# Third stage: the normalisation's DVE steps one tile later, the residual's product on DVE instead of POOL, and POOL's scatters split around the root

## The chip, the cores and the metric

One core of a Trainium2 chip (trn2) runs the whole program. The metric is the device time of one execution in microseconds (us), the median of three runs: 1230.01 us before the change (1229.64 to 1231.98). Engines: PE multiplies matrices, DVE is the vector engine, ACT the activation engine, POOL (GpSimd) also issues the indirect DMAs, SP issues the plain ones.

## The reference, cut to what matters

The layer has an attention block on 16 x 512 tokens of 128 channels, then an encoder layer with a mixture of experts. The part that matters here is the last expression:

```python
# y: [tokens, 128], after the encoder's own attention and first layer norm
idx = argmax(y @ Wg.T)                      # one of 8 experts per token
moe = relu(y @ W1[e] + b1[e]) @ W2[e] + b2[e]      # for each token its own e
z   = layer_norm(y + moe, g2, be2)
x   = x + gb * z                            # gb is kept away from zero: |gb| >= 0.25
```

## The kernel before, in words

The program has three stages: windowed attention, then the encoder's attention with routing, then the experts. The second stage scatters each token's row of 385 floats (y without the layer norm's scale, an index, x plus shift, and the gate `GC`) into a buffer in DRAM sorted by expert (L983). The third stage, from about 1048.7 us of the profiled span, is the one that the change touches.

It walks over 72 tiles (`NS`) of 128 sorted tokens, each of one expert, in 18 quads (`NQX`) of four tiles. The order is written out by hand on each engine:

- SP loads the four tiles of quad q into `xs[q % 11]`; from quad 11 on it first waits for the scatters of quad q - 11 (`s_fin`).
- PE loops over tiles t. At each even t, `turn` transposes the next pair of tiles (L1134). Then `down` of tile t - 2 (L1156, four fp32 products, results in bank `MB[k]`), then `up` of tile t (L1145 to L1147, twelve bf16 products). `up` waits for the low half of the transposed rows, `s_yl`, and for ACT to have emptied the bank of tile t - 2. `down` waits for `hx` from ACT and, with `s_b2b`, for DVE to have emptied bank k four tiles earlier.
- ACT writes `yh`, the high half of a pair (`high`, L1273), and `hx = relu(...)` (L1286).
- DVE loops over steps s, and step s handles tile t = s - 3, with q, k = divmod(t, 4). At each even s comes `low` first: the low half of a pair of tiles, t = s + 2 and s + 3 (L1455). Then the add of the expert's bias out of `MB[k]` (L1473). Then, by k: at k = 0 the scaled differences of the quad before, `(u - mean) * root`, four instructions (L1481, signals `s_cx`). At k = 1 that quad's gate product (L1487, `s_gx`) and the sum with x (L1491, `s_zx`). At k = 3 the sum of the quad's four tiles with the residual `yg` (L1495, `s_ux`), the statistics (L1501) and their aggregation (L1505, `s_sx`).
- POOL, once per quad q: the residual's product for quad q + 1, `yg = xs * g1` (L991, `s_yg`); the root of quad q, that is variance + eps (L1003) and the power -0.5 (L1005, `s_rx`), after waiting for `s_sx`; then, after waiting for `s_zx`, four indirect DMAs that scatter the rows of quad q - 1 to the output (L1010). POOL ends with a wait for all of them.

Names used below: root(q) is L1003 and L1005 of quad q, diff(q) L1481, gate(q) L1487, sum(q) L1491, stats(q) L1501 and L1505.

Of the kernel before, what the change touches and what calls it, by code (L numbers as in the profile page):

```python
# [9 lines left out]
U32 = mybir.dt.uint32  # L10
ALU = mybir.AluOpType
# [3 lines left out]
P = 128  # L15
NB, T, C = 16, 512, 128
# [4 lines left out]
NS = NT + NE  # L21
RW = 3 * C + 1
IX, XC, GC = C, C + 1, 2 * C + 1
# [698 lines left out]
def phase2(nc, a, out, top, sbt, sem, banks, x1_d, xs_d, keep, debug):  # L722
    ident, identb, b1t, modp, bc, wfa, con, rows, trf, bkf, s_l2 = keep
# [107 lines left out]
    yg = hc  # L831
    s_yg = sem("s_yg")
# [17 lines left out]
    NX, NF = NR, 4  # L850
    xs = [rr[:, 4 * n:4 * n + 4, :] for n in range(NX)]
    yh = [sbt(p2, f"yh{n}", [P, 2 * P], BF) for n in range(2)]
    yl = [sbt(p2, f"yl{n}", [P, 2 * P], BF) for n in range(2)]
    hx, ux, zx, ox = va, h2[0:2], h2[2:4], h2[4:7]
# [12 lines left out]
    s_xs = [sem(f"s_xs{n}") for n in range(NX)]  # L867
# [23 lines left out]
    with nc.Block() as blk:  # L891
# [36 lines left out]
        @blk.gpsimd  # L928
        def _(pool):
            pool.memset(nhalf[:, :], -0.5).then_inc(s_po, 1)  # L930
            for t in mv:
                pool.memset(t[:, :, :, :], 0.0).then_inc(s_po, 1)
            for k in range(NG):
                pool.memset(pw[:, k:k + 1], float(NE ** k)).then_inc(s_pw, 1)
            pool.memset(xnh[:, :], -0.5).then_inc(s_rx, 1)
            pool.memset(pad[:, :], 0.0).then_inc(s_pz, 1)
            pool.wait_ge(s_pz, 1)
            pool.memset(pad[:, IX:IX + 1].bitcast(I32), OOB).then_inc(s_pz, 1)
            pool.wait_ge(s_l2, 16 * 6)
            for n in range(2):  # L940
                pool.tensor_tensor(gg[:, n, :], modp[:, 2 * C:], bc[:, 2 + n, :], ALU.mult).then_inc(s_po, 1)
            pool.wait_ge(s_po, 5)
            n = 0
            for s in range(FIRST, LAST):
                if quad(s + 2) or quad(s - 4):
                    m, r, z = mv[s % 2], rs[s % 2][:, :, :], nb[s % 2][:, :, :]
                    if quad(s + 2):
                        pool.wait_ge(s_b1, 8 * (s + 2) + 8)
                    if quad(s - 4):
                        pool.wait_ge(s_b2, 8 * (s - 4) + 8)  # L950
                    if quad(s):
                        pool.wait_ge(s_cn, s + 1)
                    if quad(s - 6):
                        pool.wait_ge(s_cy, s - 5)
                    pool.tensor_scalar(r, m[:, :, :, 1], EPS, None, ALU.add).then_inc(s_ln, 1)
                    pool.tensor_scalar(z, m[:, :, :, 0], -1.0, None, ALU.mult).then_inc(s_ln, 1)
                    pool.wait_ge(s_ln, n + 2)
                    pool.tensor_tensor(r, r, nhalf[:, :].rearrange("p (a b) -> p a b", a=2), ALU.pow).then_inc(s_ln, 1)
                    pool.wait_ge(s_ln, n + 3)
                    pool.tensor_tensor(z, z, r, ALU.mult).then_inc(s_ln, 1)  # L960
                    n += 4
                u = s
                if quad(u):
                    x = quad_rows(u)[:, :, XC:XC + C]
                    pool.wait_ge(s_cn, u + 1)
                    pool.tensor_tensor(x, x, gg[:, 1:2, :].to_broadcast([P, 4, C]), ALU.add).then_inc(s_c0, 1)
                u = s - 1
                if quad(u):
                    pool.wait_ge(s_ri, u + 1)
                    t = pp[u % 2][:, :, :].rearrange("p h (j k) -> p (h j) k", j=4)  # L970
                    pool.tensor_tensor(t, t, ri[u % 2][:, :].unsqueeze(2).to_broadcast([P, 16, 32]), ALU.mult)\
                        .then_inc(s_nm, 1)
                u = s - 6
                if quad(u):
                    pool.wait_ge(s_sl, u + 1)
                    pool.wait_ge(s_cy, u + 1)
                    pool.wait_ge(s_ix, u + 1)
                    pool.wait_ge(s_c0, u + 1)
                    if u < NR:
                        pool.wait_ge(s_fl[u % 2], 16 * (u // 2 + 1))  # L980
                    for k in range(4):
                        t = 4 * u + k
                        pool.indirect_dma_start(out=xs_d[:, :], out_offset=bass.IndirectOffsetOnAxis(  # L983
                            ap=slot[:, t:t + 1].bitcast(U32), axis=0), in_=quad_rows(u)[:, k, :], in_offset=None,
                            bounds_check=NE * STR - 1, oob_is_err=False).then_inc(s_sca[u % 4], 16)

            def residual(q):
                pool.wait_ge(s_xs[q % NX], 64 * (q // NX + 1))
                if q >= 2:
                    pool.wait_ge(s_ux, q - 1)  # L990
                pool.tensor_tensor(yg[q % 2][:, :, :], xs[q % NX][:, :, 0:C], bc[:, 0:1, :].to_broadcast([P, 4, C]),  # L991
                                   ALU.mult).then_inc(s_yg, 1)

            residual(0)
            for q in range(NQX + 1):
                if q + 1 < NQX:
                    residual(q + 1)
                if q < NQX:
                    pool.wait_ge(s_sx, 4 * q + 4)
                    if q >= 2:  # L1000
                        pool.wait_ge(s_cx, q - 1)
                    pool.wait_ge(s_rx, 2 * q + 1)
                    pool.tensor_scalar(xrs[q % 2][:, :], xmv[q % 2][:, :, 1], EPS, None, ALU.add).then_inc(s_rx, 1)  # L1003
                    pool.wait_ge(s_rx, 2 * q + 2)
                    pool.tensor_tensor(xrs[q % 2][:, :], xrs[q % 2][:, :], xnh[:, :], ALU.pow).then_inc(s_rx, 1)  # L1005
                if q >= 1:
                    w = q - 1
                    pool.wait_ge(s_zx, w + 1)
                    for k in range(4):
                        pool.indirect_dma_start(out=out[:, :], out_offset=bass.IndirectOffsetOnAxis(  # L1010
                            ap=xs[w % NX][:, k, IX:IX + 1].bitcast(U32), axis=0), in_=ox[w % 3][:, k, :], in_offset=None,
                            bounds_check=NB * T - 1, oob_is_err=False).then_inc(s_fin[w % NF], 16)
            for h in range(NF):
                pool.wait_ge(s_fin[h], 64 * len(range(h, NQX, NF)))

# [275 lines left out]
        def _(dve):  # L1291
# [166 lines left out]
            dve.wait_ge(s_te, 1)  # L1458
            words = expert_words(mybir.EngineType.DVE)
            low(0)  # L1460
            for s in range(NS + 6):
                if s % 2 == 0 and s + 2 < NS:
                    low(s // 2 + 1)
                t = s - 3
# [2 lines left out]
                if 0 <= t < NS:  # L1467
                    if t == 0:
                        dve.wait_ge(s_b2a, 1)
                    if k == 0 and q >= 2:  # L1470
# [1 line left out]
                    dve.wait_ge(s_m2, t + 1)  # L1472
                    dve.tensor_tensor(u[:, k, :], MB[k][:, 0:C], b2r[:, bass.ds(expert(words, t) * C, C)],  # L1473
                                      ALU.add).then_inc(s_b2b, 1)
                if k == 0 and 1 <= q <= NQX:
                    v = ux[(q - 1) % 2]
                    dve.wait_ge(s_rx, 2 * q + 1)
                    if q >= 3:
                        dve.wait_ge(s_zx, q - 2)
                    for j in range(4):  # L1480
                        ins = dve.tensor_scalar(z[:, j, :], v[:, j, :], xmv[(q - 1) % 2][:, j, 0:1],  # L1481
                                                xrs[(q - 1) % 2][:, j:j + 1], ALU.subtract, ALU.mult)
                    ins.then_inc(s_cx, 1)
                if k == 1 and 1 <= q <= NQX:
                    x = xs[(q - 1) % NX]
                    dve.wait_ge(s_cx, q)
                    dve.tensor_tensor(z[:, :, :], z[:, :, :], x[:, :, GC:GC + C], ALU.mult).then_inc(s_gx, 1)  # L1487
                    dve.wait_ge(s_gx, q)
                    if q >= 4:
                        dve.wait_ge(s_fin[(q - 4) % NF], 64 * ((q - 4) // NF + 1))  # L1490
                    dve.tensor_tensor(o[:, :, :], z[:, :, :], x[:, :, XC:XC + C], ALU.add).then_inc(s_zx, 1)  # L1491
                if k == 3 and 0 <= q < NQX:
                    dve.wait_ge(s_b2b, 4 * q + 4)
                    dve.wait_ge(s_yg, q + 1)
                    dve.tensor_tensor(u[:, :, :], u[:, :, :], yg[q % 2][:, :, :], ALU.add).then_inc(s_ux, 1)  # L1495
                    dve.wait_ge(s_ux, q + 1)
                    if q >= 2:
                        dve.wait_ge(s_rx, 2 * q - 1)
                        dve.wait_ge(s_cx, q - 1)
                    for j in range(4):  # L1500
                        ins = dve.bn_stats(xst[q % 2][:, j, :], u[:, j, :])  # L1501
                    ins.then_inc(s_st, 1)
                    dve.wait_ge(s_st, q + 1)
                    for j in range(4):
                        dve.bn_aggr(xmv[q % 2][:, j, :], xst[q % 2][:, j, :]).then_inc(s_sx, 1)  # L1505
# [67 lines left out]
```

## Time and profile before

| what | value |
|---|---|
| median of three runs | 1230.01 us |
| the profiled execution: own time / span | 1225.95 us / 1224.1 us |
| third stage, first transpose to last scatter's issue | 1048.69 to 1215.56 us |
| POOL in the stage: scatters L1010, residual L991, root L1005 | 80.7, 21.6, 18.8 us |
| DVE waits for the root before L1481, 18 times | 36.7 us |
| PE busy over the whole span | 90% |

Rows of a timeline give start, duration, engine, line, operation, tiles; a bracket at the end is the idle time before it and what ended it. Times are microseconds from the span's start, unless marked ns.

### The profile page before, as it was taken

What the parts mean: (1) busy time and instruction counts of PE and PEld (TensorE: products, weight loads), DVE (VectorE), ACT (ScalarE), POOL (GpSimd) and SP (SyncE); (2) the same over time, 40 slices, a digit from 0 to 9 for tenths busy, and PEclk for the clock granted to TensorE, in tenths of its full rate; (3) what the DMA queues carried; (4) which work ended last, traced back from release to release, by engine and by line L of the source; (5) the groups of instructions that cost most, each with busy time, mean ns of one, the idle gap of its engine ahead of it and who ended that gap; (6) DMA issues with size and microseconds to landing.
All of it is one profiled execution on the core that took longest, in us unless ns stands there. A gap on an engine that the chain in (4) does not pass through costs nothing. (4 is left out here: it accounts for less than half of the span.)

```text
span 1224.1 us, 49591 instructions
## 1 busy us (share of the span) xinstructions
PE 1099.8 (90%) x17489; PEld 898.3 (73%) x17489; DVE 958.7 (78%) x4172; ACT 922.7 (75%) x3404; POOL 874.6 (71%) x703
## 2 busy tenths in 40 slices
PE   4799999999999999999999999947999972799991
PEld 2688888888888888888888887725877772688881
DVE  6898898998898898898988987546888854376763
ACT  2789989989989889899899897836877641466660
POOL 2777877877877877877777875554677776178885
PEclk9999999999999999999999999969989975799996
DMA  6776766766766666767667666353242124574100
GB/s 197 207 179 158 183 165 167 185 167 161 182 165 172 171 173 166 179 158 181 166 163 183 156 159 180 92 183 93 63 135 92 71 85 161 161 202 138 58 32 25
DMA packets 111027, 180.88 MB, mean 148 GB/s; under 512 B 19726, under 2 KB 64177, under 8 KB 110656
## 3 DMA queue, kind: packets, MB, share of 16 engines
q1 hardware_dynamic: 102944, 158.53, 50.1%
q0 software_dynamic: 6400, 16.82, 3.8%
q8 instruction: 144, 2.36, 0.9%
q10 hardware_dynamic: 1440, 2.36, 0.8%
q14 instruction: 99, 0.81, 0.2%
HBM read 35.20 MB, written 24.73 MB: 49 GB/s over the span
## 5 line engine op out<-in xcount | busy, mean ns | idle before, releaser
L612 POOL TENSOR_TENSOR qk<-mm,sw 128x1024 f32<-128x1024 f32 x128 | 305.1, 2384 | 103.2 <-DMA sw<-mm 102.6
L685 ACT ACTIVATE pr<-sm,mn 128x96 f32<-128x96 f32 x1024 | 368.7, 370 | 0.3 <-DVE mn L513 0.3
L618 POOL TENSOR_TENSOR pr<-pr,ri 128x768 f32<-128x768 f32 x128 | 189.2, 1478 | 66.7 <-DVE ri L540 66.6
L501 DVE TENSOR_TENSOR mm<-bank,cos 128x512 f32<-128x512 f32 x256 | 175.3, 685 | 70.1 <-PE bank L324 58.3
L685 ACT ACTIVATION_READ_ACCUMULATOR pr<-sm,mn 128x1 f32 x1024 | 201.6, 197 | 0.0
L513 DVE CUSTOM_DVE_ANT_0 sm<-bank,msk 128x96 f32<-128x96 f32 x1024 | 190.9, 251 | 3.4 <-PE bank L350 3.4
L502 DVE TENSOR_TENSOR mm<-bank,sin 128x512 f32<-128x512 f32 x256 | 173.8, 679 | 0.0
L377 PE MATMUL bank<-pT,vw 96*64 96x64 f32 x4096 | 148.2, 226 | 0.0
L377 PEld LDWEIGHTS bank<-pT,vw 96*64 96x64 f32 x4096 | 130.6, 138 | 17.2 <-issue 6.0
L676 ACT ACTIVATE pT<-bank 96x512 f32<-96x512 f32 x256 | 137.3, 588 | 0.2 <-PE bank L392 0.2
L392 PE MATMUL bank<-ident,pr 128*96 128x128 f32 x1024 | 133.1, 273 | 0.0
L350 PEld LDWEIGHTS bank<-qk 64*64 64x64 f32 x4096 | 91.0, 134 | 53.8 <-issue 52.5
L392 PEld LDWEIGHTS bank<-ident,pr 128*96 128x96 f32 x1024 | 115.9, 126 | 19.0 <-issue 0.2
L1286 ACT ACTIVATE fv<-bank,b1t 128x128 f32<-128x128 f32 x288 | 82.4, 368 | 54.4 <-PE bank L1147 52.9
L350 PE MATMUL bank<-qk 64*64 64x96 f32 x4096 | 115.3, 251 | 7.4 <-POOL qk L612 7.4
L322 PE MATMUL bank<-xh,wh 128*128 128x512 f32 x256 | 113.1, 442 | 2.1 <-DVE xl L426 1.4
L696 ACT ACTIVATE oth<-bank 128x512 fp32r<-128x512 f32 x128 | 76.3, 596 | 48.2 <-PE bank L377 48.2
L709 ACT ACTIVATE vn<-bank 128x512 f32<-128x512 f32 x128 | 76.2, 595 | 45.1 <-PE bank L300 45.1
L324 PE MATMUL bank<-xh,wl 128*128 128x512 f32 x256 | 101.8, 398 | 0.0
L323 PE MATMUL bank<-xl,wh 128*128 128x512 f32 x256 | 101.4, 396 | 0.0
L1010 POOL DMA_INDIRECT out<-h,rr x72 | 80.7, 1121 | 20.1 <-issue 19.8
L546 DVE TENSOR_TENSOR otl<-bank,oth 128x512 fp32r<-128x512 f32 x128 | 85.4, 668 | 9.5 <-ACT oth L696 9.4
(206 smaller groups left out, 2485.6 us busy)
## 6 DMA issues: line engine op xcount, KB each, us to landing
sw<-mm SPq DMA_DIRECT2D x512, 128.0 KB, 2.4
vw<-vn SPq DMA_DIRECT2D x128, 192.0 KB, 2.6
vw<-vn SPq DMA_DIRECT2D x128, 128.0 KB, 2.3
rr<-sorted_scratch SPq DMA_DIRECT2D x72, 192.5 KB, 2.6
vw<-vn SPq DMA_DIRECT2D x96, 64.0 KB, 2.2
xt<-in_x SPq DMA_DIRECT2D x16, 256.0 KB, 4.2
x_scratch<-x SPq DMA_DIRECT2D x16, 256.0 KB, 2.6
rr<-x_scratch SPq DMA_DIRECT2D x16, 256.0 KB, 3.2
```

The costliest lines, as they stand in the source:

```text
L322: pe.matmul(dst[:, :], wh[:, o:o + P], xh[b % 2][:, :], start=True, stop=False)
L324: pe.matmul(dst[:, :], wl[:, o:o + P], xh[b % 2][:, :], start=False, stop=True).then_inc(s_pj, 1)
L350: ins = pe.matmul(SC[h][64 * e:64 * e + 64, p * WK:(p + 1) * WK], t[r, 0, 32 + 64 * w:96 + 64 * w], t[r, 1, 64 * w:64 * w + WK], start=Tru ...
L377: ins = pe.matmul(OB[64 * h:64 * h + 64, 64 * w:64 * w + 64], vw[half % 2][:, w, c:c + 64], pT[i % 2][:, h, 64 * w:64 * w + 64], start=Tru ...
L392: ins = pe.transpose(TR[h][0:WK, p * P:(p + 1) * P], pr[i % 2][:, h, p, :], ident[:, :])
L501: dve.tensor_tensor(mm[s % 2][:, 0, j, :], PJ[u % 2][:, :], cos[:, :], ALU.mult)
L502: dve.tensor_tensor(mm[s % 2][:, 1, j, :], PJ[u % 2][:, :], sin[:, :], ALU.mult)\
L513: ins = dve.tensor_tensor_reduce(ms_[i % 2][:, h, p, :], SC[h][:, p * WK:(p + 1) * WK], msk[:, min(p, 1), :], 1.0, 3.0e38, ALU.add, ALU.mi ...
L612: pool.tensor_tensor(qk[i % 2][:, :, 32:], mm[i % 2][:, 0, :, :], sw[i % 2][:, :, :], ALU.add)\
L618: pool.tensor_tensor(t, t, ri[i % 2][:, :].unsqueeze(2).to_broadcast([P, 8, WK]), ALU.mult)\
L676: act.activation(pT[i % 2][:, h, :], TR[h][0:WK, :], ACT.Copy).then_inc(s_te, 1)
L685: ins = act.activation(pr[i % 2][:, h, p, :], ms_[i % 2][:, h, p, :], ACT.Exp, scale=-1.0, bias=mn[i % 2][:, h, p:p + 1], accum_out=sums[i ...
```

## The change

DVE's steps move by one tile: the scaled differences from k = 0 to k = 1, gate product and sum with x from k = 1 to k = 2. The residual's product leaves POOL and stands on DVE at k = 0 of its own quad, after the bias add. The loop gets one more step (`NS + 7`). On POOL the order within a quad is now: wait for `s_zx` of quad q - 1, its first two scatters, root of quad q, its other two scatters. What is computed is the same.

```diff
-            def residual(q):
-                pool.wait_ge(s_xs[q % NX], 64 * (q // NX + 1))
-                if q >= 2:
-                    pool.wait_ge(s_ux, q - 1)
-                pool.tensor_tensor(yg[q % 2][:, :, :], xs[q % NX][:, :, 0:C], bc[:, 0:1, :].to_broadcast([P, 4, C]),
-                                   ALU.mult).then_inc(s_yg, 1)
-
-            residual(0)
+            def scatter(w, k):
+                pool.indirect_dma_start(out=out[:, :], ...).then_inc(s_fin[w % NF], 16)
+
             for q in range(NQX + 1):
-                if q + 1 < NQX:
-                    residual(q + 1)
+                if q >= 1:
+                    pool.wait_ge(s_zx, q)
+                    for k in range(2):
+                        scatter(q - 1, k)
                 if q < NQX:
                     pool.wait_ge(s_sx, 4 * q + 4)
 ...
                 if q >= 1:
-                    w = q - 1
-                    pool.wait_ge(s_zx, w + 1)
-                    for k in range(4):
-                        pool.indirect_dma_start(out=out[:, :], ...).then_inc(s_fin[w % NF], 16)
+                    for k in range(2, 4):
+                        scatter(q - 1, k)
...
-            for s in range(NS + 6):
+            for s in range(NS + 7):
...
-                if k == 0 and 1 <= q <= NQX:
+                if k == 1 and 1 <= q <= NQX:
                     v = ux[(q - 1) % 2]
 ...
-                if k == 1 and 1 <= q <= NQX:
+                if k == 2 and 1 <= q <= NQX:
                     x = xs[(q - 1) % NX]
 ...
+                if k == 0 and 0 <= q < NQX:
+                    dve.wait_ge(s_xs[q % NX], 64 * (q // NX + 1))
+                    if q >= 2:
+                        dve.wait_ge(s_ux, q - 1)
+                    dve.tensor_tensor(yg[q % 2][:, :, :], xs[q % NX][:, :, 0:C], bc[:, 0:1, :].to_broadcast([P, 4, C]),
+                                      ALU.mult).then_inc(s_yg, 1)
```

## Rows read from the trace of the kernel before

**Rows 1.** Busy time by stretch: span, busy time (instructions) of each engine, clock, DMA.
```profile
core 0: us, PE busy (x) PEld busy (x) DVE busy (x) ACT busy (x) POOL busy (x), PEclk, DMA share, GB/s
1139.45:1147.67 8.22, 8.21 (x86) 7.13 (x85) 5.86 (x21) 5.12 (x18) 7.02 (x8) 1.00 0.09 32
```

**Rows 2.** Timeline of POOL, one quad from root to root.
```profile
1139.45 0.26 POOL L1003 TENSOR_SCALAR xrs<-xmv 128x4 f32<-128x4 f32 x1
1139.79 1.04 POOL L1005 TENSOR_TENSOR xrs<-xrs,xnh 128x4 f32<-128x4 f32 x1
1141.03 1.15 POOL L1010 DMA_INDIRECT out<-h,rr  x1 [0.20 <-issue]
1142.49 1.47 POOL L1010 DMA_INDIRECT out<-h,rr  x1 [0.30 <-issue]
...
1145.54 0.97 POOL L1010 DMA_INDIRECT out<-h,rr  x1 [0.30 <-issue]
1146.52 1.22 POOL L991 TENSOR_TENSOR hc<-rr,bc 128x512 f32<-128x512 f32 x1
1147.67 0.26 POOL L1003 TENSOR_SCALAR xrs<-xmv 128x4 f32<-128x4 f32 x1
```

**Rows 3.** Timeline of DVE in the same quad.
```profile
1140.87 1.11 DVE L1481 TENSOR_SCALAR h<-h,xmv,xrs 128x128 f32<-128x128 f32 x4 [2.31 <-POOL xrs L1005]
...
1142.43 0.68 DVE L1487 TENSOR_TENSOR h<-h,rr 128x512 f32<-128x512 f32 x1
1143.15 0.69 DVE L1491 TENSOR_TENSOR h<-h,rr 128x512 f32<-128x512 f32 x1
...
1144.60 0.69 DVE L1495 TENSOR_TENSOR h<-h,hc 128x512 f32<-128x512 f32 x1
...
1146.23 0.38 DVE L1505 BATCH_NORM_AGGREGATE xmv<-xst 128x2 f32<-128x6 f32 x4
1146.58 0.29 DVE L1473 TENSOR_TENSOR h<-bank,b2r 128x128 f32<-128x128 f32 x1
```

**Rows 4.** Groups of instructions from 1000 us on: what DVE waited for.
```profile
L1481 DVE TENSOR_SCALAR h<-h,xmv,xrs 128x128 f32<-128x128 f32 x72 | 21.1, 355 | 36.7 <-POOL xrs L1005 36.7
```

**Rows 5.** Timeline of PE: the transposes of pairs 8, 16, 19 and 35.
```profile
1076.98 0.41 PE L1134 MATMUL bank<-ident,rr 128*128 128x128 f32 x2
...
1108.82 0.41 PE L1134 MATMUL bank<-ident,rr 128*128 128x128 f32 x2
...
1120.89 0.41 PE L1134 MATMUL bank<-ident,rr 128*128 128x128 f32 x2
...
1186.78 0.41 PE L1134 MATMUL bank<-ident,rr 128*128 128x128 f32 x2
```

**Rows 6.** Timelines of PE and ACT: a pair's transpose and its high half.
```profile
1065.10 0.41 PE L1134 MATMUL bank<-ident,rr 128*128 128x128 f32 x2
...
1066.49 0.39 ACT L1273 ACTIVATE yh<-bank 128x256 bf16<-128x256 f32 x1
```

**Rows 7.** Timeline of DVE and POOL, the one place where L991 met L1481.
```profile
1066.94 1.17 POOL L991 TENSOR_TENSOR hc<-rr,bc 128x512 f32<-128x512 f32 x1
1066.99 1.98 DVE L1481 TENSOR_SCALAR h<-h,xmv,xrs 128x128 f32<-128x128 f32 x4 [1.30 <-POOL xrs L1005]
```

**Rows 8.** Timeline of PE and DVE: the last down product and DVE's last stats.
```profile
1196.47 1.15 PE L1156 MATMUL bank<-w,fv 128*128 x8 [0.37 <-ACT fv L1286]
...
1198.46 1.11 DVE L1481 TENSOR_SCALAR h<-h,xmv,xrs 128x128 f32<-128x128 f32 x4 [2.54 <-POOL xrs L1005]
...
1203.18 0.38 DVE L1505 BATCH_NORM_AGGREGATE xmv<-xst 128x2 f32<-128x6 f32 x4
```

**Rows 9.** Timeline of POOL at the end.
```profile
1203.79 0.25 POOL L1003 TENSOR_SCALAR xrs<-xmv 128x4 f32<-128x4 f32 x1
...
1205.36 1.14 POOL L1010 DMA_INDIRECT out<-h,rr  x1 [0.20 <-issue]
...
1213.31 0.97 POOL L1010 DMA_INDIRECT out<-h,rr  x1 [0.30 <-issue]
1214.59 0.97 POOL L1010 DMA_INDIRECT out<-h,rr  x1 [0.30 <-issue]
```

More of the change, by code:

```diff
@@ L985, in _ @@
                             bounds_check=NE * STR - 1, oob_is_err=False).then_inc(s_sca[u % 4], 16)
-            def residual(q):
-                pool.wait_ge(s_xs[q % NX], 64 * (q // NX + 1))
-                if q >= 2:
-                    pool.wait_ge(s_ux, q - 1)
-                pool.tensor_tensor(yg[q % 2][:, :, :], xs[q % NX][:, :, 0:C], bc[:, 0:1, :].to_broadcast([P, 4, C]),
-                                   ALU.mult).then_inc(s_yg, 1)
-            residual(0)
+            def scatter(w, k):
+                pool.indirect_dma_start(out=out[:, :], out_offset=bass.IndirectOffsetOnAxis(
+                    ap=xs[w % NX][:, k, IX:IX + 1].bitcast(U32), axis=0), in_=ox[w % 3][:, k, :], in_offset=None,
+                    bounds_check=NB * T - 1, oob_is_err=False).then_inc(s_fin[w % NF], 16)
             for q in range(NQX + 1):
-                if q + 1 < NQX:
-                    residual(q + 1)
+                if q >= 1:
+                    pool.wait_ge(s_zx, q)
+                    for k in range(2):
+                        scatter(q - 1, k)
                 if q < NQX:
@@ L1006, in _ @@
                 if q >= 1:
-                    w = q - 1
-                    pool.wait_ge(s_zx, w + 1)
-                    for k in range(4):
-                        pool.indirect_dma_start(out=out[:, :], out_offset=bass.IndirectOffsetOnAxis(
-                            ap=xs[w % NX][:, k, IX:IX + 1].bitcast(U32), axis=0), in_=ox[w % 3][:, k, :], in_offset=None,
-                            bounds_check=NB * T - 1, oob_is_err=False).then_inc(s_fin[w % NF], 16)
+                    for k in range(2, 4):
+                        scatter(q - 1, k)
             for h in range(NF):
```

## The prediction, made before the changed kernel ran

> **What bounds the kernel now.** I read the page's forty slices first, then the groups of the last stretch, the timelines of POOL, DVE and PE for one quad, and last the end of the timeline. The chain of waits holds only POOL's last scatters and says no more than that POOL ends the program. In a late quad, POOL is busy for 7.02 of 8.22 us and the rest is the gap in front of each scatter, so it never stops [rows 1]. Its rows close on themselves: root 1139.45 to 1140.83, four scatters 1141.03 to 1146.51, residual to 1147.67, root again [rows 2]. DVE has work for 5.86 us and then waits 2.31 us for the root [rows 1, 3], 36.7 us over the 18 quads [rows 4]. So POOL sets the pace there, at 8.22 us a quad.
>
> PE looks just as full, and a full PE is not a PE at its peak. Its transposes tell its pace. From pair 8 to pair 16 it needs 31.84 us for 8 pairs, 3.98 us each, or 7.96 a quad. From pair 19 to pair 35 it needs 65.89 us for 16, 4.12 each, or 8.24 a quad, which is POOL's pace [rows 5]. PE runs at its own pace until POOL's lag has used up the banks and buffers between them, and is then held through DVE: the low halves stand behind L1481 in DVE's order, and `up` waits for them. What POOL can give back in the loop is therefore 0.26 to 0.28 us a quad and no more, for PE is the next bound.
>
> The end is another matter. The last down product ends at 1197.62 [rows 8], yet DVE is still waiting for root(16) until 1198.46, so stats(17) end at 1203.56. Root(17) comes next, and then eight scatters in a row, four of quad 16 and four of quad 17, from 1205.36 to 1215.56 [rows 8, 9]. From there to the end of the span are 8.5 us in which no engine works; I take them as unchanged.
>
> **The change part by part.**
>
> *Residual off POOL.* 18 instructions, each worth 1.15 us from start to the next start (1146.52 to 1147.67) [rows 2]. POOL's own work falls from 8.22 to 7.07 us a quad, below PE's 7.96.
>
> *Residual onto DVE.* The trace has this shape on DVE only in its sisters L1487 and L1495: 128x512, 0.68 and 0.69 us, 0.72 from start to start [rows 3]. I take 0.72. The bound below is 0.29 (an add of a quarter of the size) [rows 3], the bound above 1.2, POOL's own duration for it. DVE's work becomes 5.91 + 0.72 = 6.6 us a quad (8.22 less the wait of 2.31), under 7.96; the wait for the root, which goes, covers it. Its wait for the quad's rows costs nothing, as PE has transposed the same rows some two tiles earlier. Its wait on `s_ux` is for DVE's own earlier work. Behind it on DVE's queue stand the next `low` and, through it, PE's `up`; `low` finds its input only about 1.8 us after the transpose (1065.10 to 1066.88) [rows 6], and the product ends before that.
>
> *Differences, gate and sum one tile later.* No instruction is added. The order gives the root a full tile: stats(q), add, product, the low half, add, and only then diff(q). The banks see the same adds and the wait for `s_b2b` four tiles back has slack. The output buffers are freed as before, since only four quads back are asked for. SP's loads of quads 11 to 17 hang on scatters of quads 0 to 6, long before PE needs them: no cost.
>
> *Scatters around the root.* Four scatters as before, but two of them leave the stretch behind the root, two come before it. They now wait for sum(q-1) before root(q) may run, a new wait: behind it on POOL stand the root and the other two scatters, and DVE's diff waits for the root. So I walk the ring. After sum(q-1) ends, DVE does low, add, L1495, stats: 2.77 us (1143.84 to 1146.61) [rows 3]. POOL does two scatters meanwhile, 2.6 us at the clean spacing of 1.28 [rows 9], up to 3.2 where each meets DVE's long operations (1.15 and 1.47 plus 0.30 each) [rows 2]. Root 1.38 us. Then diff, add, gate, sum: 2.97 less the low half of 0.34 among them, 2.6 [rows 3]. Sum: 2.8 to 3.2 + 1.4 + 2.6 = 6.8 to 7.2, plus hand-overs of 0.1 to 0.2 each, about 7.2.
>
> *The ports.* Where L991 had just started on POOL, the four instructions of L1481 took 1.98 instead of 1.11 us; in reverse, the scatter that starts under L1487 takes 1.47 instead of 0.97 us [rows 2, 3, 7]. The new product on DVE is issued about 0.25 us after the stats end, just when the root starts on POOL. If it is let through between L1003 and L1005, the power waits for it, up to 0.7 us: the ring becomes 7.2 + 0.6 = 7.8. If the power is first, the product waits for it. I take the first, because the root's first instruction can't start before the stats end and takes 0.34 us to the second's start (1139.45 to 1139.79) [rows 2], while the product needs only the add of 0.25.
> The Trainium skill, "SBUF — State Buffer", section "Who interferes with whom", states this as a rule: a VectorE instruction with two inputs in SBUF contends with a GpSimd instruction that reads SBUF, and whoever issues first holds the shared pair for its whole length. By that rule the moved product doesn't leave POOL for free, and the ring is 7.8 (or, the other way round, the second rival below); without it, 7.2. L1481 under L991, 1.98 us for 1.11, agrees. Both are under PE's 7.96, so the forecast holds either way.
>
> *The sum.* The loop first: from pair 16 to pair 35 are 19 pairs, 77.96 us [rows 5]. At 3.98 they take 75.62, so the last transpose comes 2.34 earlier, at 1184.44. From it, the end:
> - low half from 1186.25, diff(15) from 1186.9, sum(15) ends at 1189.5, stats(16) at 1192.0 (2.77 less a low half);
> - POOL scatters two of quad 15, 1189.7 to 1192.3; root(16) with half of the possible blocking, to 1194.1;
> - diff, gate, sum(16): 1196.75. Stats(17): 1199.2, with PE's last product long done (1197.62 less at least the loop's 2.34). POOL meanwhile two scatters of quad 15 to 1197.2 (1141.03 to 1143.96 is 2.93) and, from 1197.5, two of quad 16, to 1200.2;
> - root(17) to 1201.7; two of quad 16 to 1204.8; four of quad 17 at 1.28 from 1205.1, the last done at 1209.9.
>
> Before, it was done at 1215.56. That is 5.7 us less: 2.3 from the loop, 2.6 from two scatters that no longer stand behind the last root (2 x 1.28), and 0.8 from DVE's not being held at the end. The span goes to 1218.4, the profiled execution's own time from 1225.95 to 1220.3. The median of the runs shown lies 4.06 above the profiled execution; I subtract from it: 1230.01 - 5.7 = 1224.3.
>
> **The rivals.**
> 1. *The ring, not PE, sets the pace.* If scatters meet long operations in both pairs (3.2 each) and the power is blocked, the ring is 3.2 + 0.7 + 1.4 + 2.6 + hand-overs of 0.3, that is 8.2, today's pace. Only the two scatters at the end are won: 1230.01 - 2.56 = 1227.4. For it: POOL's second scatter takes 1.47 in nearly every quad. Against it: the fourth, under the stats, takes 0.97 [rows 2].
> 2. *Slower: the power holds the product.* If root and product meet the other way in each quad, DVE's product ends 0.7 after the root, and low, add and diff come after it, where the plan has diff right behind the root: 2.8 + 0.1 + 1.4 + 0.7 + 0.35 + 0.3 + 2.6 + 0.3 = 8.6 us a quad. From the end of root(0) at about 1066.9 to that of root(17), 1203.79 + 1.37, are 138.2 us today, 8.13 a quad [rows 7, 9]; 17 x (8.6 - 8.13) = 8.0, less 2.56: 5.4 slower, 1235.4. It decides as soon as the add at k = 0 is late by over 0.2 us, so that the power starts first. Against it: PE runs ahead of DVE, whose stats close a quad 2.8 us after its sum, so the bank of that add is full before DVE comes to it.
> 3. *PE's slower second half isn't POOL's doing.* Then the loop gives nothing and the end 3.4: 1226.6. For it: PE waits on nothing in those rows by name. Against it: 8.24 against POOL's 8.22 is no accident.
>
> **How the numbers follow.** Forecast 0.67, rival 1 0.15, rival 2 0.07, rival 3 0.11. The forecast's own spread: PE at 3.93 a pair would give 0.95 more and clean scatters 0.9, so 1222.4; all hand-overs late, 1225.8. The range goes on to rivals 3 and 1 and a little over at the top, 1221.6 to 1228.2. A measurement tells 0.2%, 2.5 us, from no change: the border is 1227.55. Forecast, rival 3 and under half of rival 1 lie below it: 0.84 faster, 0.09 within, 0.07 slower.
>
> **What would show it.** Transposes of pairs 19 to 35 at 3.98 us apart; POOL with idle time before its first scatter or its root; DVE's wait before L1481's successor near zero; six scatters behind the last root instead of eight; the root's power at over 1.04 us, or the product at over 0.72, where they meet. I am wrong if a quad still takes 8.2 us or more while POOL idles, or if the last scatter isn't issued by about 1212.

## The result and the profile after

The changed kernel takes 1224.19 us, median of 12 runs (1221.48 to 1228.69), against 1229.83 for 12 runs of the kernel before: ratio 0.9949, 95% interval 0.9932 to 0.9967. That is 5.6 us less and clear of 0.2%; forecast were 5.7 and 1224.3 us.

The two profiled spans, 1224.1 and 1223.0 us, don't show it: in the second one the two stages that the change doesn't touch happened to take 4.48 us longer (first transpose of the third stage at 1053.17 instead of 1048.69). A third trace, of the kernel before, has it at 1051.73, so this start moves by some us from run to run. I therefore compare from the first transpose to the end of the last scatter: 166.87 us before, 161.27 after, 5.60 less.

The transposes of pairs 8, 16, 19 and 35 after, from PE's timeline, answer to [rows 5] (the lines of the code have moved; L1129 was L1134):

```profile
1082.30 0.41 PE L1129 MATMUL bank<-ident,rr 128*128 128x128 f32 x2
...
1114.15 0.41 PE L1129 MATMUL bank<-ident,rr 128*128 128x128 f32 x2
...
1126.02 0.41 PE L1129 MATMUL bank<-ident,rr 128*128 128x128 f32 x2
...
1189.70 0.41 PE L1129 MATMUL bank<-ident,rr 128*128 128x128 f32 x2
```

Pairs 8 to 16 are 3.98 us apart, as before; pairs 19 to 35 are now 3.98 too, where it was 4.12. PE no longer slows down in the second half. The busy time of one quad, answering to [rows 1]:

```profile
core 0: us, PE busy (x) PEld busy (x) DVE busy (x) ACT busy (x) POOL busy (x), PEclk, DMA share, GB/s
1141.97:1149.98 8.01, 7.94 (x86) 7.08 (x85) 6.66 (x24) 5.11 (x18) 5.99 (x7) 1.00 0.10 35
```

PE stays full at 7.94 of 8.01 us; POOL has gone from 7.02 to 5.99.

POOL's timeline over two quads, answering to [rows 2] (L988 is the scatter, L1002 and L1004 the root):

```profile
1142.52 0.77 POOL L1002 TENSOR_SCALAR xrs<-xmv 128x4 f32<-128x4 f32 x1 [0.45 <-DVE xmv L1506]
1143.38 1.04 POOL L1004 TENSOR_TENSOR xrs<-xrs,xnh 128x4 f32<-128x4 f32 x1
1144.62 1.14 POOL L988 DMA_INDIRECT out<-h,rr  x1 [0.20 <-issue]
1146.07 1.15 POOL L988 DMA_INDIRECT out<-h,rr  x1 [0.30 <-issue]
1147.89 0.97 POOL L988 DMA_INDIRECT out<-h,rr  x1 [0.68 <-issue]
1149.17 0.97 POOL L988 DMA_INDIRECT out<-h,rr  x1 [0.31 <-issue]
1150.41 0.23 POOL L1002 TENSOR_SCALAR xrs<-xmv 128x4 f32<-128x4 f32 x1 [0.27 <-DVE xmv L1506]
1150.72 1.35 POOL L1004 TENSOR_TENSOR xrs<-xrs,xnh 128x4 f32<-128x4 f32 x1
```

And DVE's in the same place, answering to [rows 3] (L1491 is the moved product, L1476, L1482, L1486 are differences, gate and sum):

```profile
1142.52 0.68 DVE L1491 TENSOR_TENSOR hc<-rr,bc 128x512 f32<-128x512 f32 x1
1143.77 0.42 DVE L1450 TENSOR_TENSOR yl<-bank,yh 128x256 bf16<-128x256 f32 x1 [0.57 <-ACT yh L1268]
...
1144.46 1.12 DVE L1476 TENSOR_SCALAR h<-h,xmv,xrs 128x128 f32<-128x128 f32 x4
...
1146.41 0.69 DVE L1486 TENSOR_TENSOR h<-h,rr 128x512 f32<-128x512 f32 x1
...
1149.94 0.38 DVE L1506 BATCH_NORM_AGGREGATE xmv<-xst 128x2 f32<-128x6 f32 x4
...
1150.49 0.68 DVE L1491 TENSOR_TENSOR hc<-rr,bc 128x512 f32<-128x512 f32 x1
```

Three things are to be read here. POOL now idles before its root and is released by DVE's statistics, a bracket that a late quad of [rows 2] doesn't have. DVE's differences start with no wait; over the stage the wait for the root is 3.9 us where it was 36.7 [rows 4]. And product and root do meet: in one quad L1491 and L1002 start together and L1002 takes 0.77 us instead of 0.26, in the next L1491 starts 0.08 us behind L1002, while it still runs, and L1004 takes 1.35 instead of 1.04. The product itself stays at 0.68.

The end of POOL's timeline, answering to [rows 9]:

```profile
1204.88 0.26 POOL L1002 TENSOR_SCALAR xrs<-xmv 128x4 f32<-128x4 f32 x1
...
1206.46 1.15 POOL L988 DMA_INDIRECT out<-h,rr  x1 [0.20 <-issue]
...
1209.66 0.97 POOL L988 DMA_INDIRECT out<-h,rr  x1 [0.68 <-issue]
...
1213.47 0.97 POOL L988 DMA_INDIRECT out<-h,rr  x1 [0.30 <-issue]
```

Six scatters stand behind the last root instead of eight. From the last transpose to the end of the last scatter are 24.74 us (1189.70 to 1214.44), 28.78 before.

### The profile page after: what moved, and what is told of

It is laid out like the page before. It is cut to its first block and busy times, and to the rows that moved or that the text cites. A ratio compares the mean times of both kernels' runs of the same rounds, so it can differ in the third digit from the quotient of the medians.

```text
span 1223.0 us, 49591 instructions
## 1 busy us (share of the span) xinstructions
PE 1102.8 (90%) x17489; PEld 902.1 (74%) x17489; DVE 971.2 (79%) x4190; ACT 921.4 (75%) x3404; POOL 854.5 (70%) x685
## 5 line engine op out<-in xcount | busy, mean ns | idle before, releaser
L988 POOL DMA_INDIRECT out<-h,rr x72 | 76.6, 1064 | 31.0 <-issue 26.1
```

## The experiments

One table first. "16 to 35" is the time between those transposes, "end" the time from the last transpose to the end of the last scatter, "stage" from the first transpose to there, each from the one profiled execution; the ratio is to the kernel before on the same chip; "-" stands where the chip isn't on record. The experiments ran on three chips. On two of them, 11 and 15, every kernel was slower (the kernel before at 1278 and 1273 us), and all traces from there but that of "product on POOL" have stops of ACT and PE that the others don't have. Times from these two chips can't be set beside those of the others. Nor does one trace stand for its kernel there: "product on POOL" was traced in the fastest of its twelve executions (1251.34 us, median 1261.43), "not later" in the second slowest of twelve (1275.91, median 1266.29), "product at k = 2" in the fastest of twelve (1249.61, median 1264.26).

| run | chip | 16 to 35 | end | stage | ratio (95%) |
|---|---|---|---|---|---|
| before | - | 77.96 | 28.78 | 166.87 | |
| before again | 7 | 77.76 | 28.68 | 166.56 | |
| changed | - | 75.55 | 24.74 | 161.27 | 0.9949 (0.9932 to 0.9967) |
| product alone, 3rd | 7 | 75.59 | 26.96 | 163.27 | 0.9949 (0.9930 to 0.9968) |
| no split, 3rd | 7 | 75.65 | 26.43 | 162.94 | 0.9967 (0.9947 to 0.9987) |
| product twice | 7 | 75.55 | 25.93 | 161.90 | 0.9939 (0.9915 to 0.9962) |
| product alone, 1st | 11 | 101.11 | 28.10 | 203.54 | 1.0206 (1.0146 to 1.0266) |
| no split, 1st | 11 | 108.03 | 27.09 | 210.08 | 1.0163 (1.0090 to 1.0236) |
| product on POOL | 11 | 76.93 | 27.32 | 166.46 | 0.9913 (0.9871 to 0.9954) |
| not later | 11 | 84.43 | 26.78 | 175.41 | 0.9930 (0.9894 to 0.9967) |
| changed again | 15 | 82.55 | 25.48 | 171.98 | 0.9915 (0.9877 to 0.9953) |
| product alone, 2nd | 15 | 105.16 | 28.07 | 206.11 | 1.0235 (1.0187 to 1.0282) |
| no split, 2nd | 15 | 107.86 | 29.32 | 210.23 | 1.0193 (1.0139 to 1.0247) |
| product at k = 2 | 15 | 84.58 | 24.82 | 172.96 | 0.9928 (0.9898 to 0.9958) |

**Product alone.** The kernel before, with only the product moved: POOL's `residual` and its two calls go, and DVE gets the product behind the scaled differences at k = 0.

```diff
--- before
-            residual(0)
-                if q + 1 < NQX:
-                    residual(q + 1)
+                if k == 0 and 0 <= q < NQX:
+                    dve.wait_ge(s_xs[q % NX], 64 * (q // NX + 1))
+                    ...
+                    dve.tensor_tensor(yg[q % 2][:, :, :], xs[q % NX][:, :, 0:C], ..., ALU.mult).then_inc(s_yg, 1)
```

Expected, first run:

> Only the residual's product moves to DVE (k = 0, behind the scaled differences, which stay at k = 0); the four scatters stay behind the root. Theory A (the order counts: DVE must not wait for the root it has just fed): DVE's own quad becomes a ring of stats, root 1.45 with the hand-over, differences 1.05, product 0.72, two low halves 0.68, adds 1.1, gate and sum 1.43, L1495 and stats 1.98, that is 8.1 to 8.4 us a quad, about today's 8.13; eight scatters still stand behind the last root, so 0 to 1 us less than before (ratio 0.999 to 1.000). Theory B (POOL's load alone counts, 1.15 us a quad less on POOL is enough): PE's pace of 3.98 us a pair and the whole gain of some 5.6 us (ratio 0.9955).

Second run:

> Only the product moved, once more beside the changed kernel, since PE's own issue was uneven in the first run. Theory A (the order counts): a ring on DVE of 8.1 to 8.4 us a quad with DVE waiting 1.3 to 1.5 us for every root, 4.05 to 4.2 us a pair, about 28 us from the last transpose to the last scatter: 0 to 1 us less than before, 5 us more than the changed kernel. Theory B (POOL's load alone counts): 3.98 us a pair and as fast as the changed kernel.

Third run:

> Only the product moved to DVE, a third time for the same reason. Theory A (the order counts): DVE waits 1.2 to 1.5 us for every root, a quad on DVE is 8.0 to 8.4 us, pairs 4.0 to 4.2, 28 us behind the last transpose: 0 to 1 us less than before (ratio 0.999 to 1.000). Theory B (POOL's load alone counts): pairs 3.98 and the changed kernel's ratio, 0.995. Theory C: pairs over 4.3 and slower than before.

The first two runs met neither theory: 2.1% and 2.4% slower than the kernel before, with the stops of chips 11 and 15 (see "What stays open"). On chip 7 theory A fell. The loop has all of its gain from the product alone: 75.59 us for 19 pairs, as in the changed kernel, though DVE waits 1.23 to 1.31 us for the root in the quads shown and 22.7 us in all. Its timeline there:

```profile
1152.09 0.23 POOL L993 TENSOR_SCALAR xrs<-xmv 128x4 f32<-128x4 f32 x1 [1.36 <-DVE xmv L1501]
1152.40 1.04 POOL L995 TENSOR_TENSOR xrs<-xrs,xnh 128x4 f32<-128x4 f32 x1
1153.48 1.11 DVE L1471 TENSOR_SCALAR h<-h,xmv,xrs 128x128 f32<-128x128 f32 x4 [1.23 <-POOL xrs L995]
...
1154.51 0.68 DVE L1486 TENSOR_TENSOR hc<-rr,bc 128x512 f32<-128x512 f32 x1
...
1161.39 1.12 DVE L1471 TENSOR_SCALAR h<-h,xmv,xrs 128x128 f32<-128x128 f32 x4 [1.31 <-POOL xrs L995]
```

From differences to differences are 7.91 us. I had added up durations of 8.1 to 8.4; start to start the steps are shorter, and the sum lies just under PE's 7.96. Over the first fifteen quads it is 7.86 to 8.25, 7.96 on average, and in eleven of them DVE stands for nothing but the root: PE doesn't feel DVE's wait, but less than 0.1 us a quad is left. Theory B was right on the loop, and its ratio of 0.995 was met. In the stage 2.0 us are missing to the changed kernel (163.27 against 161.27), nearly all of it at the end: 26.96 against 24.74.

**No split.** The changed kernel with the four scatters together behind the root.

```diff
--- after
-                if q >= 1:
-                    pool.wait_ge(s_zx, q)
-                    for k in range(2):
-                        scatter(q - 1, k)
                 if q < NQX:
                     ...
                 if q >= 1:
-                    for k in range(2, 4):
-                        scatter(q - 1, k)
+                    w = q - 1
+                    pool.wait_ge(s_zx, w + 1)
+                    for k in range(4):
+                        ...
```

> The changed kernel with the four scatters of a quad together behind the root again; product and later steps as in the change. Theory A: the loop keeps 3.98 us a pair, since the ring through POOL is no longer than before. At the end eight scatters stand behind the last root again, but that root needs no scatters ahead of it and comes earlier, so the walk through the end gives about 1.1 us more than the changed kernel (4.5 less than before, ratio 0.9964). As the prediction booked it (2 x 1.28 us for the two scatters): 2.6 us more than the changed kernel (ratio 0.998). Theory B: as the changed kernel.

> The changed kernel with the four scatters together behind the root, once more beside the changed kernel. Theory A (walk through the end): 3.98 us a pair, the stretch behind the last transpose 1.1 us longer than the changed kernel's 24.7, and no 0.79 us hand-over from the sum to a scatter in the loop. As the prediction booked it: 2.6 us longer. If the split carried the loop as well, the pairs would go to 4.1.

> The changed kernel without the split (four scatters together behind the root), a third time, because the chips of its first two runs stopped ACT and PE for 1 to 5 us at a time, the last chip did not. Where the pairs keep 3.98 us, theory A asks for a stretch behind the last transpose 1.1 us longer than the changed kernel's 24.7 (ratio to before 0.996); the prediction's booking asks for 2.6 longer (ratio 0.997). Theory C (four scatters in a row hold ACT and PE up whatever the chip): pairs over 4.3 and slower than before.

The first two runs were again slower than the kernel before, by 1.6% and 1.9%. On chip 7 the loop keeps 75.65, so the split does nothing for the loop there. The end is 26.43, 1.7 us longer than with the split: between the walk's 1.1 and the 2.6 that the prediction booked. The timings can't tell these: 0.9967 and 0.9949 have overlapping intervals.

**Product back on POOL.** The changed kernel, steps later and split as in the change, with `residual` on POOL again.

```diff
--- after
             for q in range(NQX + 1):
+                if q + 1 < NQX:
+                    residual(q + 1)
                 if q >= 1:
                     pool.wait_ge(s_zx, q)
...
-                if k == 0 and 0 <= q < NQX:
-                    (the product on DVE)
```

> The changed kernel with the residual's product back on POOL, ahead of the quad's first two scatters; later steps and split as in the change. Theory A: POOL's quad is again 8.2 to 8.3 us and sets the pace in the second half (pairs 19 to 35 about 4.12 us apart), DVE's wait for the root stays near zero because of the later steps; only the end gains, 1 to 2.6 us less than before (ratio 0.998 to 0.999). Theory B: no gain at all (ratio 1.000).

POOL's product comes every 8.12 us, so POOL sets the pace again, at nearly the 8.22 us of [rows 1]. What the other two edits are worth without the product's move isn't shown. The stage takes 166.46 us, only 0.4 less than the kernel before in its first trace, where 1 to 2.6 were expected; but that trace is from another chip. The ratio of 0.9913 on its own chip is a gain of some 11 us, which neither theory expected; the kernel before has no trace there that could explain it, and the changed kernel has no time there. DVE's wait for the root, which I expected near zero, is 23.3 us. This kernel also shows the ports best, in one quad of both engines:

```profile
1171.02 1.19 POOL L991 TENSOR_TENSOR hc<-rr,bc 128x512 f32<-128x512 f32 x1
1171.44 1.33 DVE L1500 TENSOR_TENSOR h<-h,hc 128x512 f32<-128x512 f32 x1
...
1179.14 1.20 POOL L991 TENSOR_TENSOR hc<-rr,bc 128x512 f32<-128x512 f32 x1
```

DVE's sum with two inputs in SBUF, 0.69 us elsewhere [rows 3], takes 1.33 under POOL's product, in thirteen of the 18 quads.

**Not later.** The changed kernel with differences at k = 0, gate and sum at k = 1, as before.

```diff
--- after
-            for s in range(NS + 7):
+            for s in range(NS + 6):
-                if k == 1 and 1 <= q <= NQX:
+                if k == 0 and 1 <= q <= NQX:
-                if k == 2 and 1 <= q <= NQX:
+                if k == 1 and 1 <= q <= NQX:
```

> The changed kernel with differences back at k = 0 and gate and sum at k = 1; product on DVE and split as in the change. Theory A: the ring sum, 0.79 to the first scatter, two scatters 2.6, root 1.4, differences 1.05, product 0.72, low half and add 0.65, gate and sum 1.43 is 8.3 to 8.7 us a quad, longer than today's 8.13 and than PE's 7.96, so this is 0 to 7 us slower than before (ratio 1.000 to 1.006), DVE waiting for the root in every quad. Theory B (POOL's load alone counts): the whole gain, ratio 0.9955.

The steps of the ring that I had written down are there. From the timelines of POOL and DVE in one quad:

```profile
1181.86 0.69 DVE L1486 TENSOR_TENSOR h<-h,rr 128x512 f32<-128x512 f32 x1
...
1183.35 0.97 POOL L988 DMA_INDIRECT out<-h,rr  x1 [1.78 <-DVE h L1486]
1183.64 0.42 DVE L1450 TENSOR_TENSOR yl<-bank,yh 128x256 bf16<-128x256 f32 x1 [0.89 <-ACT yh L1268]
...
1184.62 1.21 POOL L988 DMA_INDIRECT out<-h,rr  x1 [0.30 <-issue]
...
1185.93 0.38 DVE L1506 BATCH_NORM_AGGREGATE xmv<-xst 128x2 f32<-128x6 f32 x4
1186.40 0.23 POOL L1002 TENSOR_SCALAR xrs<-xmv 128x4 f32<-128x4 f32 x1 [0.57 <-DVE xmv L1506]
1186.72 1.04 POOL L1004 TENSOR_TENSOR xrs<-xrs,xnh 128x4 f32<-128x4 f32 x1
1187.80 1.12 DVE L1476 TENSOR_SCALAR h<-h,xmv,xrs 128x128 f32<-128x128 f32 x4 [1.31 <-POOL xrs L1004]
```

The sum ends at 1182.55, the scatter starts 0.80 later, and two scatters end at 1185.83. But the root doesn't start then: it waits 0.57 us more, for DVE's statistics, in nearly every quad, and these are late because DVE has waited 0.89 for ACT's high half. A pair takes 4.44 us (84.43 / 19), 8.9 a quad, above the 8.3 to 8.7 of theory A, and these rows show that the ring through the scatters isn't what sets it. Its own steps add up to 8.3 us, an estimate: 3.28 from the sum to the end of the second scatter, 0.03 to the root, 1.40 from there to the differences (1186.40 to 1187.80) and 3.57 from there to the next sum's end at 1191.37. That is theory A's figure and over PE's 7.96, so on a chip without stops this kernel could well be held at 8.3; no run shows it. The ratio of 0.993 stands against theory A's 1.000 to 1.006; whether the kernel before is itself held up on this chip isn't shown, as it has no trace there.

**Changed kernel again**, unedited, for the comparison on chip 15.

> The changed kernel once more, as it is, as the measure for the three beside it on the same chip: 3.98 us a pair, 24.7 us from the last transpose to the last scatter, 161.3 us from the first transpose to the last scatter; about 5.6 us less than before.

The end is 25.48, near the first trace's; the loop isn't 3.98 but 4.34 a pair, with the chip's stops in it.

**Product at k = 2.** The changed kernel with one condition changed, so that the product stands behind the sum with x.

```diff
--- after
-                if k == 0 and 0 <= q < NQX:
+                if k == 2 and 0 <= q < NQX:
                     dve.wait_ge(s_xs[q % NX], 64 * (q // NX + 1))
```

> The changed kernel with the product at k = 2, behind the sum with x, instead of k = 0, so that it no longer meets the root on POOL. Theory A (port): L1002 and L1004's successors go back from 0.77 and 1.35 to 0.25 and 1.04 us in every quad, which is 0.3 to 0.5 us less per root, but the pace stays PE's 3.98 us a pair, and the end gains at most 0.5: 0 to 0.5 us less than the changed kernel, within noise. Rival (the DVE-POOL ring sets the pace): the product now stands between the sum and the statistics, the ring grows by 0.7 and the pairs go to 4.1 or more.

Root instructions over the whole stage, of this kernel (groups of instructions):

```profile
L1004 POOL TENSOR_TENSOR xrs<-xrs,xnh 128x4 f32<-128x4 f32 x18 | 18.8, 1043 | 1.5
...
L1002 POOL TENSOR_SCALAR xrs<-xmv 128x4 f32<-128x4 f32 x18 | 4.2, 234 | 50.5 <-DVE xmv L1506 50.3 <-issue 0.2
```

and of the changed kernel:

```profile
L1004 POOL TENSOR_TENSOR xrs<-xrs,xnh 128x4 f32<-128x4 f32 x18 | 21.2, 1177 | 1.5
L1002 POOL TENSOR_SCALAR xrs<-xmv 128x4 f32<-128x4 f32 x18 | 7.8, 433 | 35.0 <-DVE xmv L1506 34.8
```

Out of each other's way, both take what they took before: 6.0 us less on POOL over 18 roots, 0.33 each. The time doesn't move: 0.9928 beside 0.9915 for the changed kernel. Pairs are 4.45 us apart, 4.34 in the changed kernel on this chip; the rival asked for 4.1 or more, but with the chip's stops the pace decides nothing here. The meeting of product and root is real and costs nothing that lasts, since POOL idles anyway.

**Before again**, unedited, for its trace.

> The kernel before, once more, for its trace beside the experiments: in the first traces its pairs are 3.98 us apart at first and 4.12 us from pair 19 on. In the two runs with product on DVE and four scatters in a row (the product moved alone; the change without the split), pairs went to 5.2 to 5.7 us, with PE standing once a quad after the third or fourth scatter. Theory C (four scatters in a row hold ACT and PE up): this kernel, which also has four in a row, shows the same stops and pairs well over 4.3 us. Theory A (order of POOL and DVE alone): pairs at 4.1 us, POOL never idle, no such stops.

On chip 7 it repeats the first trace: 3.98 us, then 4.11 a pair, stage 166.56. Theory C isn't supported there: four scatters in a row don't stop anybody on this chip, here or in the two kernels above.

**Product twice.** The changed kernel with the product computed a second time behind the first, the same values.

```diff
--- after
+                    dve.tensor_tensor(yg[q % 2][:, :, :], ..., ALU.mult).then_inc(s_y2, 1)
+                    dve.wait_ge(s_y2, q + 1)
                     dve.tensor_tensor(yg[q % 2][:, :, :], ..., ALU.mult).then_inc(s_yg, 1)
```

> The changed kernel with the product computed twice on DVE (0.7 us more of DVE a quad, in series). It measures the slack. Theory A (PE sets the pace; DVE's work is 6.6 of 7.96 us and the ring from sum to sum 7.1 to 7.8): 7.3 of 7.96 on DVE, pairs stay within 0.1 of the changed kernel's, and the end grows by 0.7 to 1.4: within 0.15% of the changed kernel's ratio. Rival (the DVE-POOL ring sets the pace): 0.7 us a quad more, some 12 us, 1% slower than the changed kernel.

The loop takes exactly the same 75.55 us; the end is 1.2 longer. The ratio is 0.9939, against 0.9949. DVE and the ring had over 0.7 us a quad to spare, so the pace is set on PE's side, where PE is busy for 7.94 of 8.01 us: rival 1 is out, and so is rival 2, whose product would have been late here if anywhere.

## Why the prediction was right

*PE's own pace is the next bound: right.* Forecast 75.62 us for pairs 16 to 35, measured 75.55, and again 75.55 with twice the product. Rival 3, that the slower second half had another cause, is out: it went with nothing but POOL's product moved.

*DVE takes the product in: right.* Forecast 0.72 from start to start; busy 0.68, and DVE is busy 6.6 us of a quad, as forecast (13.23 us in two quads of the changed trace). The 1.15 us that POOL gives up cost DVE 0.7 under cover.

*The later steps are what hides the root: right as a mechanism, worth almost nothing by itself.* The wait went from 36.7 to 3.9 us. But with the product alone the wait of 22.7 us that stays sits inside PE's 7.96. What the later steps may do is make room for the split, whose two scatters would otherwise stand between sum and root: the ring is then 8.3 us by the estimate above, which no run measured free of stops. The prediction treated the three edits as one and didn't say so.

*The ring: right in its size, wrong in one part.* Near the end, where no tile of PE's paces it, it can be read from root to root: 1199.13 to 1206.26 (ends of the power), 7.13 us against 7.2, with the last root 0.02 us behind the second scatter. Inside, I booked hand-overs of 0.1 to 0.2 us each. From the sum's end to the scatter are 0.79 (1147.10 to 1147.89), and other steps were shorter.

*The ports: right, with less force.* I let the product through ahead of the power. In eight quads the power is held so, 1.31 to 1.35 us for 1.04; in seven others the root's first instruction is, 0.57 to 0.78 us for 0.23; in the last three neither. Either way POOL loses 0.3 to 0.5, not up to 0.7, and the product takes 0.71 at most where it meets the root: the root never holds it, as rival 2 had it. That L1002 and L1004 are held by an instruction with two SBUF inputs agrees with the rule that the prediction names (the Trainium skill, "SBUF — State Buffer", section "Who interferes with whom"); L1500 under POOL's product, 1.33 us for 0.69, does too. L1481, which the prediction counts for it, is no such case: it takes one tensor and two scalars per partition. That POOL's idle time swallows the delay isn't in the rule.

*The end: 4.0 us gained where 3.3 were booked,* and the split's own term was too large. The 2.56 us for two scatters are, between the changed kernel and the one without the split, 1.7. The six scatters behind the last root take 7.98 us, the eight without the split 10.14, which is 2.2 and not 2.56, since the third of the six waits 0.68 for the last sum instead of 0.30. And without the split the last root starts 0.5 earlier (14.71 us behind the last transpose, 15.18 with it). Moving the product alone gives 1.8 (28.78 to 26.96), as the last root starts 15.26 us behind the last transpose and not 17.01; the later steps 0.5. So the end's sum is 1.8 + 0.5 + 1.7, where I had 0.8 and 2.6.

*What I hadn't booked: 0.85 us lost at the start.* From the first transpose to pair 16 are 60.98 us, 60.13 before. The windows of PE show TensorE's granted clock:

```profile
core 0: us, PE busy (x), PEclk, DMA share, GB/s
1058.17:1059.17 1.00, 1.00 (x6) 0.50 0.71 192
1059.17:1060.17 1.00, 1.00 (x8) 0.50 0.74 180
1060.17:1061.17 1.00, 1.00 (x13) 0.63 0.53 149
```

It is 0.50 (1.2 GHz) until past 1060.17, 7.0 us after the first transpose; in the kernel before it was 0.99 in the window from 6.0 to 7.0 us. PE had stood idle for 20.57 us ahead of its first transpose and 20.55 before. The clock of 0.63 in the window from 7.0 to 8.0 us puts the rise at 7.7 us, some 1.7 later than before, and 1.7 us at half the clock cost about 0.85, an estimate that accounts for the whole loss. Other traces speak for chance and against the change: the same changed kernel, traced again on chip 15, has 0.77 already in the window from 4.0 to 5.0 us, and its first eight pairs take 28.33 us, where the first trace has 29.13 and the kernel before 28.29. Over all the traces the rise comes between 4 and 8 us behind the first transpose.

So the total of 5.6 against 5.7, in these two traces, holds with two errors that cancel: 0.7 more at the end, 0.85 less at the start. That they are of one size is luck; the loop's 2.4 is not.

## What stays open

On chips 11 and 15 the two kernels that combine the product on DVE with four scatters in a row lost 21 to 30 us to the kernel before, in two runs each, while the kernels with two and two gained 9 to 11. In their traces ACT stands still for some us, up to 5, about once a quad, and PE waits for it (ACT's timeline of the product-alone kernel on chip 15, then PE's; what "remote" stands for, the trace doesn't say):

```profile
1185.64 0.63 ACT L1276 ACTIVATE fv<-bank,b1t 128x128 f32<-128x128 f32 x2
1191.09 1.14 ACT L1276 ACTIVATE fv<-bank,b1t 128x128 f32<-128x128 f32 x4 [4.83 <-remote]
```

```profile
1192.37 0.82 PE L1146 MATMUL bank<-w,fv 128*128 x5 [3.41 <-ACT fv L1276]
```

Of the 18 stops of PE over 0.6 us in that trace, all but two begin after the third or fourth scatter of a quad. The kernel before has four in a row too, and its 1273 to 1278 us there leave it less room for such stops; no trace of it was taken on these chips. That bursts of scatters bring the stops on is thus only a pattern, and on chip 7 the same two kernels have none. Another fits as well: the only kernel traced on these chips with the product still on POOL is also the only one almost without stops (two of PE over 0.3 us, 1.3 us in all; 15 to 20 of them, 10 to 13 us, in the others with two and two; 23 to 27, 33 to 37 us, with four in a row). What differs between the chips isn't known.

## What to carry to other kernels

Look for the engine that never idles in the steady stretch, and then for the pace that the next one showed while there was still slack: pairs 8 to 16 gave the new pace to 0.1% before anything was changed. On chip 7, moving one instruction off the bound engine gave the whole gain of the loop and two thirds of that of the stage; putting steps later, which took DVE's wait for the root from 22.7 to 3.3 us, gave 0.5 us, because the wait lay under PE. On chips 11 and 15 that one move alone made the kernel slower, and only the kernels with the split gained, so a change is worth trying whole and in parts on more than one chip. Compare a stage from its own first instruction to its last: the spans differed by 1.1 us where the stage differed by 5.6.

## What the runs showed of the hardware that I hadn't expected

An indirect DMA on POOL that waits for DVE starts 0.79 us after DVE's instruction ends (1147.10 to 1147.89, and again 1208.87 to 1209.66 at the end; 0.80 in the "not later" kernel, where POOL had stood idle), while scatters that wait for nothing start 0.30 us after the one before. And the same kernel can be faster than the one before on one chip and 2% slower on another: 0.9949 against 1.0206 and 1.0235 for the product alone.
